# First layer's attention in rounded parts: scores and weighted values 256 wide in three passes, groups of two sequences, the outputs' weights split in place

## The reference, cut to what matters

```
qkv = silu(xn @ qkv_w.T)                      # q, k, v of each head: 256 x 128
scores = einsum(q, k) * decay                 # causal, decayed
attn = einsum(scores, v)                      # 256 x 128
xf = attn * rsqrt(mean(attn * attn) + EPS)    # over all 32 heads
gate = sigmoid(xn @ gate_w.T)
out = (gate * norm_w * xf) @ out_w.T
```

## Time and profile before

| | |
|---|---|
| median of 3 runs | 2571.38 us (2569.98 to 2574.78) |
| the profiled execution's own time | 2570.18 us |
| its span, first to last instruction | 2568.3 us |
| PE, weight loads, DVE, ACT, POOL busy | 97%, 83%, 46%, 45%, 59% |
| mean granted clock of PE | 0.991 of full |

### The profile page before, as it was taken

How to read it: one execution, slowest core, us unless ns; L and a number is a source line. 1 busy time by engine, 2 the same in 40 slices (tenths; PEclk the granted TensorE clock), 3 DMA queues, 4 the chain that set the end, 5 groups by cost and what they waited for, 6 DMA issues and landing times.

```text
span 2568.3 us, 39435 instructions
## 1 busy us (share of the span) xinstructions
PE 2495.5 (97%) x13338; PEld 2140.1 (83%) x13338; DVE 1172.4 (46%) x1937; ACT 1152.2 (45%) x2182; POOL 1508.9 (59%) x1523
## 2 busy tenths in 40 slices
PE   7999999999999999999999999999999999969999
PEld 6888888888888888778888888888888888857777
DVE  6333333434343435763334343434343588865443
ACT  5444444444444444443444444444444457733332
POOL 5756656666575754765666766757575578731210
PEclk9999999999999999999999999999999999979999
DMA  4211110111111112211111011111111178931100
GB/s 166 87 48 40 55 63 31 63 47 61 36 58 47 56 40 99 94 48 48 40 55 63 31 63 47 59 35 61 47 56 40 60 245 305 301 101 34 37 29 33
DMA packets 84950, 188.00 MB, mean 73 GB/s; under 512 B 12610, under 2 KB 30674, under 8 KB 84870
## 3 DMA queue, kind: packets, MB, share of 16 engines
q1 hardware_dynamic: 76326, 170.13, 20.0%
q0 software_dynamic: 8544, 16.82, 2.2%
HBM read 168.00 MB, written 26.79 MB: 76 GB/s over the span
## 4 chain that ended last, share of the span: by engine, by line
PE 85%; DVE 7%; ACT 4%; issue 2%; DMA 1%; POOL 1%; ACTq 0%; SPq 0%; DVEq 0%
PE bank L95 24%; PE bank L96 23%; PE bank L97 23%; PE bank L1081 4%; PE bank L1064 4%; PE bank L1082 2%; PE bank L1065 2%; DVE el L2201 2%; ACT exth L2161 1%; ACT eh L2172 1%; ACT eh L2166 1%; DVE ehf L2213 0%; DMA l_stage<-y_slots,slot_of 0%; POOL l_stage L2720 0%; PE bank L539 0%
## 5 line engine op out<-in xcount | busy, mean ns | idle before, releaser
L1805 POOL TENSOR_TENSOR wl<-w_in,wh 128x512 fp32r<-128x512 f32 x510 | 587.7, 1179 | 189.5 <-ACT wh L1348 183.2
L95 PE MATMUL bank<-xh,wh 128*128 128x512 f32 x1400 | 560.7, 400 | 0.7 <-ACT bank L1296 0.7
L97 PE MATMUL bank<-xh,wl 128*128 128x512 f32 x1400 | 546.6, 390 | 0.0
L1823 POOL TENSOR_TENSOR sqacc<-sqacc,sq 128x512 f32<-128x512 f32 x128 | 165.6, 1294 | 379.3 <-ACT sq L1333 368.2
L1348 ACT CAST wh<-w_in 128x512 fp32r<-128x512 f32 x502 | 263.6, 567 | 274.0 <-POOL w_in L498 274.0
L96 PE MATMUL bank<-xl_sums,wh 128*128 128x512 f32 x800 | 315.8, 395 | 0.0
L97 PEld LDWEIGHTS bank<-xh,wl 128*128 128x128 f32 x1400 | 263.0, 188 | 57.3
L95 PEld LDWEIGHTS bank<-xh,wh 128*128 128x128 f32 x1400 | 263.5, 188 | 53.4 <-ACT bank L1296 0.9
L1602 DVE TENSOR_TENSOR acc<-bank,acc 128x512 f32<-128x512 f32 x240 | 165.7, 691 | 299.6 <-PE bank L97 299.6
L95 PE MATMUL bank<-wh,xh 128*128 128x256 f32 x912 | 260.3, 285 | 3.3 <-DVE xl L550 3.3
L96 PE MATMUL bank<-wl,xh 128*128 128x256 f32 x912 | 258.4, 283 | 0.0
(11 more groups left out here) (354 smaller groups left out, 5394.4 us busy)
## 6 DMA issues: line engine op xcount, KB each, us to landing
w_in<-in_w_pairs_dram SPq DMA_DIRECT2D x100, 512.0 KB, 3.8
o_in<-in_o_pairs_dram SPq DMA_DIRECT2D x32, 512.0 KB, 4.8
eraw<-in_ex_dram SPq DMA_DIRECT2D x31, 513.0 KB, 5.1
y_slots<-ey SPq DMA_DIRECT2D x31, 512.0 KB, 6.0
w_in<-in_w_pairs_dram SPq DMA_DIRECT2D x56, 256.0 KB, 3.1
dcur<-in_decay_dram SPq DMA_DIRECT2D x32, 384.0 KB, 3.0
eraw<-in_ex_dram SPq DMA_DIRECT2D x31, 256.0 KB, 5.1
out_dram<-acc SPq DMA_DIRECT2D x16, 256.0 KB, 2.0
```

Of the source, the lines that this page charges most:

```text
L95: pe.matmul(out, wh, mh, start=start and i == 0, stop=False, skip_group_check=True)
L97: ins = pe.matmul(out, wl, mh, start=False, stop=stop and i == n - 1, skip_group_check=True)
L1805: pool.tensor_tensor(wl[:, cols], w_in[:, cols], wh[:, cols].bitcast(F32), ALU.subtract).then_inc(w_lo, 1)
L1823: pool.tensor_tensor(sqacc[:, c], sqacc[:, c], sq[:], ALU.add).then_inc(p_sq, 1)
```

## The change

Scores and weighted values of an item, 256 columns wide, are computed in three passes of rounded parts; the 128-wide rest stays plain fp32. The items go in groups of two sequences of one head: `pieces` is the two 128-wide score products of a group, in a bank of its own, `scores` the 256-wide ones. ACT makes the high parts (`high_kq`, `high_v`, `high_ms`), DVE the low ones, those of q, k and v in place (`low_kq`, `low_v`, `low_ms`). There is one mask for the pieces (256 columns) and one for the wide ones (512). The decays are loaded 256 columns wide instead of 384. To have room, `o_in` is put in the place of `ol`: it is loaded at the end of a round for the next unit, behind the last output product, and split in the next round (`split_o(u, ...)`, `low_o`), on POOL behind the second squares.

```diff
-            "even": {"g": 4, "v0": 8, "v1": 12, "o": 14, "q": 18, "k": 22}, "odd": {"g": 4, "q": 8, "k": 12, "o": 14},
+            "even": {"g": 4, "o": 6, "v0": 10, "v1": 14, "q": 18, "k": 22}, "odd": {"o": 2, "g": 6, "q": 10, "k": 14},
...
-    o_in = sb("o_in", [P, OCOLS])
+    qh, kh, vh = sb("qh", [P, 2, S], F32R), sb("kh", [P, 2, P], F32R), sb("vh", [P, 2, DH], F32R)
+    o_in = nc.alloc_sbuf_tensor_at("o_in", [P, OCOLS], F32, offset=ol_at)
...
     # sync, run
-                    if not r.first:
-                        wait(sp, w_lo, r.o_ready())
-                    sp.dma_start(o_in[:], o_pairs[n]).then_inc(dma_o, 16)
...
                     wait(sp, pe_p, product_n(r, 2, 4))
...
+                    sp.dma_start(o_in[:], o_pairs[n]).then_inc(dma_o, 16)
...
     # tensor
+                def pieces(u, g, r=None):
+                    hd, b = ITEMS[2 * g]
+                    if r:
+                        wait(pe, a_c, taken_n(r, "b", 0))
+                    if r is None or not r.first:
+                        wait(pe, v_mask, u * 8 + (2 * g - 1))
+                    for i in range(2):
+                        c = slice((b + i) * S + P, (b + i + 1) * S)
+                        ins = pe.matmul(sc[1][:, i * P:(i + 1) * P], kT[:, hd, c], qT[:, hd, c], start=True, stop=True)
+                    ins.then_inc(pe_s, 1)
+
+                def scores(u, g):
+                    hd, b = ITEMS[2 * g]
+                    wait(pe, v_s, u * 16 + (4 * g + 2))
+                    for i in range(2):
+                        s0 = (b + i) * S
+                        ins = three_passes(pe, sc[0][:, i * S:(i + 1) * S],
+                                           [(kh[:, i, :], k_lo[:, hd, s0:s0 + P], qh[:, i, :], q_lo[:, hd, s0:s0 + S])],
+                                           i == 0, True)
+                    ins.then_inc(pe_s, 1)
...
     # values
+                    wait(pe, v_s, u * 16 + (4 * g + 4))
...
+                        three_passes(pe, out, [(vh[:, i, :], low, msh[:, i, :], ms_lo[:, i, :])], True, False)
+                        ins = pe.matmul(out[:, P:S], v1, ms2[:, i, :], start=False, stop=True, skip_group_check=True)
...
     # tensor, run
-                        section(r, 0, 1, 5)
+                        section(r, 0, 1)
+                        pieces(r.u, 1)
+                        section(r, 0, 5)
                         values(r, 0)
-                        scores(r, 2)
-                        scores(r, 3)
-                        section(r, 0, 6, 2, 7)
+                        scores(r.u, 1)
+                        section(r, 0, 6)
+                        pieces(r.u, 2)
+                        section(r, 0, 2, 7)
                         values(r, 1)
-                        scores(r, 4)
-                        scores(r, 5)
-                        section(r, 0, 3, 4)
+                        scores(r.u, 2)
+                        section(r, 0, 3)
+                        pieces(r.u, 3)
+                        section(r, 0, 4)
                         section(r, 1, 1)
                         values(r, 2)
-                        scores(r, 6)
-                        scores(r, 7)
+                        scores(r.u, 3)
                         section(r, 1, 5)
                         project_out(r, 0)
                         section(r, 1, 6)
...
     # scalar, run
+                    if not r.first:
+                        high_v(r, 0)
+                        high_ms(u, 0)
+                        high_kq(u, 1)
                     take(r, 0, "ab")
                     take(r, 0, "t5")
...
                         square(u, 1)
                         y_high(u, 1)
+                        high_v(r, 2)
+                        high_ms(u, 2)
+                        high_kq(u, 3)
                     take(r, 0, "c")
                     if not r.end:
                         take(r, 0, "b")
+                    if not r.first:
+                        split_o(u, 0)
+                        split_o(u, 1)
...
                     if r.second:
                         split(r, "g", 0, 1)
                     take(r, 1, "ab")
                     if r.second:
                         split(r, "g", 2, 3)
                     elif r.odd:
                         split(r, "g", 0, 1)
                     elif r.even:
                         split(r, "v0", 0, 1)
...
                     if not r.first:
                         square(u, 2)
+                        high_v(r, 3)
+                        high_ms(u, 3)
                     take(r, 1, "t5")
...
                     take(r, 2, "e")
-                    if not r.first:
-                        wait(a, pe_out, r.n * 8)
-                    split_o(r.n, 0)
                     take(r, 2, "c")
-                    split_o(r.n, 1)
...
     # vector, run
+                        low_v(r, 0)
+                        low_ms(u, 0)
+                        low_kq(u, 1)
                         gated(u, 0)
-                        mask(u, 2)
-                        mask(u, 3)
+                        mask_pieces(u, 1)
+                        mask(u, 1)
                         summed(r, 0, "c")
                         y_low(u, 0)
+                        low_v(r, 1)
+                        low_ms(u, 1)
+                        low_kq(u, 2)
                         summed(r, 0, "e")
                         gated(u, 1)
...
                         gated(u, 2)
-                        mask(u, 6)
-                        mask(u, 7)
+                        mask_pieces(u, 3)
+                        mask(u, 3)
+                        low_v(r, 3)
+                        low_ms(u, 3)
...
                         add_out(u, 0)
...
     # gpsimd, run
                     if r.even:
                         add_low(r, "g")
                         add_squares(u, 1)
+                        low_o(r)
                     else:
                         add_squares(u, 1)
+                        low_o(r)
                         add_low(r, "g")
...
                     if r.even:
                         add_low(r, "v0")
...
-                    low_o(r)
```

More of the change, by code:

```diff
@@ L346 @@
               "odd": {"g": 4, "q": 8, "k": 12}}
-    READY = {"second": (-6, 0, 4, 6), "even": (-6, -2, 4, 12), "odd": (-4, 0, 4), "end": (-6, -2)}
+    READY = {"second": (-4, 0, 6, 8), "even": (-4, 0, 4, 14), "odd": (-4, 0, 6), "end": (-4, 0)}
     PLACE = {"front0": {"q": 0, "k": 1, "g": 2, "v": 3}, "front1": {"q": 0, "k": 1, "g": 2, "v": 3},
@@ L389, in o_ready @@
     def o_ready(self):
-        return self.splits - (8 if self.odd else 4 if self.second else 0)
+        return self.split("o")
     def place(self, what):
@@ L681, in front @@
         def front():
-            first = [Normed(g, ms[0][:, 64 * g:64 * g + 64]) for g in range(2)]
+            first = [Normed(g, ms[:, 0, 64 * g:64 * g + 64]) for g in range(2)]
             s_x = [[sem(f"dma_x0_{t}") for t in range(TPG)], sem("dma_x1")]
@@ L1229, in shared_out @@
                     if t == 0:
-                        wait(pe, w_lo, END.split("o"))
+                        wait(pe, w_lo, END.split("so"))
                         wait(pe, v_yl, 4 * UNITS + 2)
@@ L1354, in split_o, with high_kq @@
                     a.copy(high[:, i * D:(i + 1) * D], raw[:, i * D:(i + 1) * D]).then_inc(w_hi, 1)
+                def high_kq(u, g, r=None):
+                    hd, b = ITEMS[2 * g]
+                    if r:
+                        wait(a, a_c, taken_n(r, "b", 0))
+                    if last or g or not zero(u):
+                        wait(a, pe_s, u * 8 + 2 * g)
+                    both = [x[:, hd, b * S:(b + 2) * S].rearrange("p (i c) -> p i c", i=2) for x in (kT, qT)]
+                    a.copy(kh[:], both[0][:, :, 0:P]).then_inc(a_s, 1)
+                    a.copy(qh[:], both[1]).then_inc(a_s, 1)
+                def high_v(r, g):
+                    u = r.u
+                    hd, b = ITEMS[2 * g]
+                    if g == 0:
+                        wait(a, a_c, r.takes)
+                    if last or g or not zero(u):
+                        wait(a, pe_av, 4 * u + g)
+                    v = vt_odd[b // 2][:] if r.even or r.end else vt[:, 2 * b:2 * b + 4, :]
+                    v = v.rearrange("p (i k) c -> p i k c", k=2)[:, :, 0, hd * DH:(hd + 1) * DH]
+                    a.copy(vh[:], v).then_inc(a_s, 1)
+                def high_ms(u, g):
+                    wait(a, v_mask, u * 8 + (2 * g + 2))
+                    a.copy(msh[:], ms[:]).then_inc(a_s, 1)
                 def gates_high(g):
@@ L1395, in run @@
                         y_high(u, 0)
+                        high_v(r, 1)
+                        high_ms(u, 1)
+                        high_kq(u, 2)
                     if r.even:
@@ new lines, in mask, with low_kq @@
+                def mask(u, g):
+                    wait(v, pe_s, u * 8 + (2 * g + 2))
```

(26 more changed lines are left out.)

101 lines of the change are left out of this document (57 added, 44 removed).

## The result

The changed kernel takes 2733.94 us (median of 4 runs, 2731.25 to 2737.41), the kernel before beside it 2572.97 (2569.98 to 2574.78). The ratio is 1.0628, 95% interval 1.0608 to 1.0647: 161 us slower. The forecast was 2735.

The account below looks back on a forecast made before the run. PE's queue was taken to bound the rounds. Waits of 54.6 (odd), 86.8 (even), 10 and 1 plus 51 for the clock, less 38.4 saved, gave +165 on 2570.2: 2735 us, range 2690 to 2780 (chance 0.63).

Parts of the forecast that it names:

- the clock's term: Granted clock falls after each long wait: 1.7 us for each of 30 rounds, 51 us, bounds 0 and 60.
- PE saves: Scores and values: twelve rounded passes per group replace plain fp32 256-wide products, 38 us less PE work, bounds 36 to 40.
- an odd round loses: PE waits 3.9 us at project_out(2) in each of 14 odd rounds, 54.6 us, plus 1.7 of clock each.
- an even round loses: project_out(2) resumes 4.8 to 7.5 us late, taken 6.2, in 14 even rounds, 86.8 us, plus 1.7 of clock each.
- a second round loses: Each half's second round: PE waits 3.7 us for section 1's take and 1.4 at project_out(2), 5 us, plus clock.
- The named chain: From section 0's product 4 through outputs' weights, sums, splits and group 3 to add_out(0): 11.5 us against PE's 8.7.
- three collisions: Even rounds: DVE subtractions delayed by POOL put group 2's parts at 18 to 19 us where PE wants 16.0.
- no section to split there: Last round of a half: only the outputs' weights can be late, costing 0.5 us.
- The wait without the clock: Rival: PE pauses 2.75 us odd, 4 even, at full clock: 2626, to about 2690 with central waits; chance 0.21.
- All hidden: Rival: chain under 8.7 us or otherwise hidden, only PE's saving left, 2532 us, faster; chance 0.08.
- The passes aren't cheaper: Rival: unhidden weight loads at 256 columns make each pass take more than 0.119 us; chance counted "in with the first".
- POOL becomes the bound: Rival: POOL, locked out by DVE, makes sections' low parts late, 8 us more per round, over 2780; chance 0.06.

Follow-up runs that it names:

- e0: Kernel before, its plain 256-wide products replaced by three rounded passes each on fixed, already split operands, nothing added to other engines: 2536.42 us, ratio 0.9867.
- e2: Changed kernel with square(2), high_v(3) and high_ms(3) moved on ACT ahead of the next section's splits: 2645.98 us, ratio 1.0294.
- e3: Changed kernel with low_v(3) and low_ms(3) moved on DVE from ahead of add_out(0) to behind add_out(2): 2661.76 us, ratio 1.0357.
- e5: Changed kernel with y's high and low parts of groups 0 and 1 moved behind the next group's parts, on ACT and DVE: 2741.61 us, ratio 1.0691.
- e7: Kernel before with extra DVE reductions ahead of add_out(0) in odd rounds: three, 2577.33 us, no pause; seven, 2631.53 us, 2.19 us pauses.
- e8: Changed kernel with ACT, DVE and late-y reorderings together, POOL's sums first in second rounds, and even rounds' gate work behind the outputs' weights: 2603.09 us, ratio 1.0131.
- e9: e8 plus one wait: in even rounds POOL's low parts of v0 start only after DVE's low half of gated group 3: 2570.25 us, ratio 0.9992.
- e10: e9 with POOL waiting for one more pair of DVE operations, and the changed kernel's DVE order in the second half's second round: 2568.91 us, ratio 0.9994.

## Why the prediction was right

It was right in its range and in its mechanism, but for the clock's term in the even rounds. That it hit the time to 1 us is luck: against e0 it had the three kinds of round 17 us too long together and the rest of the kernel 15 us too short. Term by term, from the profiled executions:

| term | predicted | measured |
|---|---|---|
| PE saves | 38 | 36 (e0) |
| an odd round loses, against e0's | 3.9 + 1.7 = 5.6 | 5.2 mean (14 rounds, 72.6 in all) |
| an even round loses | 6.2 + 1.7 = 7.9 | 7.5 mean (14 rounds, 104.8 in all) |
| a second round loses | 5 + 1.7 | 5.0 and 3.3 |
| before the first second round, between the halves, after the last round | 1, and up to 3 | 5.4, 2.0 and 8.7 |

- **The odd round's wait.** The named chain (outputs' weights, sums, splits, group 3, `add_out`) is the one of the trace, 3.48 us against 3.9; e2 and e3 each cut it at another link and took it away, but for 0.3 us in e3. That ACT's and DVE's new work itself would be hidden is shown as well: the odd round of e2 does all of it in 49.03 us.
- **The even round: the wait right, the clock added where it was covered.** I had `project_out(2)` held back by 4.8 to 7.5 us, taken 6.2, and put 1.7 us of clock on top. In e5, where PE waits for `acc` in every even round, `project_out(2)` starts 25.2 us after the round's first `gated` in the first half and 26.7 in the second, 5.8 and 7.4 later than in e0 (19.4 and 19.3): the term was well sized. In the changed kernel PE first loses time at groups 1 to 3, 3.65 us of pauses and, in six of the seven rounds of the first half, a fall. It then comes to `project_out(2)` too late to wait. The first even round has no fall; there PE waits for `acc`, and the round is as long as the third, which has one (PE's timeline, then both in the table of stretches):

```profile
175.33 0.50 PE L95 MATMUL bank<-oh,yh 128*128 128x512 f32 x1 [1.34 <-DVE acc L1708]
```

```profile
150.18:225.78 75.60, 70.58 (x425) 62.00 (x424) 37.35 (x52) 38.92 (x76) 47.47 (x46) 1.00 0.13 39
281.34:356.93 75.59, 71.90 (x425) 63.28 (x424) 37.41 (x52) 38.92 (x76) 47.48 (x46) 0.98 0.14 44
```

  Time that PE loses ahead of a wait that others set is not added to it. So the sum of 7.9 was too much in the first half, where an even round loses 6.5 us against e0's; in the second half, where 4.6 to 5.4 us of pause and 6.83 us at half clock were traced, it loses 8.4. The two errors cancel in part. What I called collisions ("three collisions", 0 to 1.0 us at group 1) was sized rightly for group 1 (0.75) and was at the top of its bounds for group 2 (1.23 and 1.67).
- **The second rounds.** Both named waits are there: 3.13 and 3.21 us for ACT's take, 0.45 and 2.24 for `acc`. In the second half that 2.24 stands in the place of a wait of 5.55 us that e0 has there (5.29 in the kernel before): the wait for ACT covers the rest, which fits the smaller loss of 3.3 us.
- **The clock.** Within the span, time at the lower level rose from 44.4 us (6 stretches) to 167.3 (33): 27 more stretches, for 30 rounds with long waits. One fall costs 1.57 us (e7), 1.7 was taken. But "each" was wrong: three odd rounds of the second half had their 3.42 us pause and no fall (52.8 to 52.9 us), others had twice the length, 6.83. A chance per pause is the better form. By the Trainium skill, "TensorE: Matmul & The Clock Gate", section "HAM oscillation — how this bites in real kernels", as I had read it, every recurring wait pays; the trace agrees for 11 of the 14 odd rounds and not for these three.
  Two odd rounds of the changed kernel's second half, one with a fall and one without, in the table of stretches:

```profile
1592.55:1647.04 54.49, 51.12 (x256) 42.91 (x256) 29.90 (x48) 28.00 (x56) 33.16 (x34) 0.97 0.14 46
1724.87:1777.75 52.88, 49.47 (x256) 41.77 (x256) 29.90 (x48) 27.99 (x56) 33.72 (x34) 1.00 0.15 47
```

- **Outside these rounds** 16 us were lost that the prediction had at 4 at most. Just ahead of the first second round PE has a pause of 2.08 us for `ms_lo`, with a fall beside it. For the last round of a half I had "no section to split there" and a loss of 0.5 us. In the second half's, ACT splits other weights in that place (`split_o(UNITS, ...)`), ahead of `square(2)`: PE waits 2.35 us for `acc` at 2195.27, with a fall behind it. e3 takes this wait away and e2 leaves 0.47 of it, so it is the odd rounds' queue once more. The column adds up to the difference of the two spans, 2735.6 less e0's 2533.9: 201.7.
- **Rivals.** "The wait without the clock" would have been 2626 to 2690; e7 and the 33 stretches rule it out. "All hidden" fell at the point named, 8.7 us of PE's work against a chain of 11.6 measured from the take alone. "The passes aren't cheaper" is ruled out by e0. "POOL becomes the bound" didn't come true: POOL is busy for 31.13 and 46.78 us of the two rounds where it was 30.30 and 46.32, and PE's waits for what POOL makes are 0.3 us in all up to the last round.

## What to carry to other kernels

Before moving an operation in an engine's list, write down what is queued behind it and who waits for that: here 36 us of saved products were paid for with 200, and the same instructions in another order, with one wait more, gave 165 us back (2734 to 2569). Cure every late link of a round before judging an edit: one that moves the wait to the next link measures as worthless alone (e5) and counts once that link is cured. Price a pause by its length plus one likely fall of the clock, but never add a loss that lies ahead of a wait which other engines set.

## What was unexpected in the hardware

**DVE can be shut out for several POOL instructions in a row.** In e8 one operation with two SBUF inputs took 7.66 us where its median is 0.75, through POOL's squares, four subtractions and a sum; it ended 0.56 us after that sum's end (1329.80), where POOL's next sum follows. In e9 the next operation did the same, 6.70 us, to 0.29 after the sum's end at 1205.56; in e10, where POOL stood still from 1201.45, 2.63 us, to 0.55 after that. Elsewhere the two take turns (0.95 to 1.77 us a DVE operation in the even round shown). The Trainium skill, "SBUF — State Buffer", section "SBUF: two separate sides", has the shared pair of ports as a lock for the whole of an instruction; by that, as an estimate, a DVE operation would lose one POOL instruction's length, 1.3 us. These runs agree on the exclusion and not on the length. That POOL takes the lock again, ahead of a waiting DVE, fits all of them, but no run shows the lock itself. The seven cases of e8 and the seven of e9 begin within 1.1 us of the start of a token send of POOL's, and the first half, without sends, has none. Sends alone don't bring it: the changed kernel has as many and no operation of DVE over 2 us in its rounds. That the send has a part in it was not tried.

**A pause of 2.19 us is followed by a fall in 8 rounds of 14 (e7), one of 3.37 to 3.48 in 11 of 14 (the changed kernel)**, and the first half's even rounds, with pauses of 0.75, 1.23 and 1.67 us in all three kernels, had a fall in 6 of 7 (the changed kernel), 2 of 7 (e3) and none of 7 (e2). Length alone doesn't decide; what else does stays open.
